# Copying the gather indices on GpSimd instead of ScalarE in the three walks of a graph network

## The reference

```python
z = (x @ W).reshape(num_nodes, heads, d)
e = leaky_relu(el[src] + er[dst])            # el, er: scores of z
alpha = softmax of e over the edges of one dst
out = jax.ops.segment_sum(z[src] * alpha[:, :, None], dst, num_segments=n)   # walk 1: 2 heads, walk 2: 1 head
...
msgs = x[src] * w[:, None]
agg = jax.ops.segment_sum(msgs, dst, num_segments=n)                         # walk 3
agg = agg / jnp.maximum(wsum, 1e-06)[:, None]
```

## Time and profile before

| | |
|---|---|
| median of 3 timed runs | 4649.5 us (4644.11 to 4653.87) |
| profiled execution: span, from first to last instruction | 5278.5 us |
| profiled execution: own time beside its span | none is given other than the span |
| mean granted TensorE clock, share of full speed | 0.746 |
| busy share of the span: PE, DVE, ACT, POOL | 59%, 37%, 29%, 51% |
| walks 1, 2, 3, the stretch that holds their gathers | 1252.7, 1190.7, 1179.0 us |
| gathers in each walk | 784 |

### The profile page before, as it was taken

How to read it: one execution, slowest core, us unless ns; L and a number is a source line. 1 busy time by engine, 2 the same in 40 slices (tenths; PEclk the granted TensorE clock), 3 DMA queues, 4 the chain that set the end, 5 groups by cost and what they waited for, 6 DMA issues and landing times. The chain is left out here.

```text
span 5278.5 us, 61729 instructions
## 1 busy us (share of the span) xinstructions
PE 3093.1 (59%) x11768; PEld 1898.6 (36%) x11768; DVE 1971.5 (37%) x5574; ACT 1533.2 (29%) x4863; POOL 2683.4 (51%) x2732
## 2 busy tenths in 40 slices
PE   3245555565543454455564499911666667666699
PEld 2123233333321222222233388810333333333466
DVE  4246565555523333333336712251222222223222
ACT  2122232222221222222222133310344443434233
POOL 0366666666626666666653145525666666661121
PEclk9667776767766777767775699965777777777899
DMA  5346566666623333333335266684444444442111
GB/s 152 84 97 104 107 107 109 106 110 106 107 53 97 98 95 97 99 96 97 99 87 150 76 204 218 223 234 125 118 118 122 120 122 120 123 121 60 63 57 49
DMA packets 381422, 598.24 MB, mean 113 GB/s; under 512 B 102442, under 2 KB 272078, under 8 KB 380658
## 3 DMA queue, kind: packets, MB, share of 16 engines
q0 software_dynamic: 136000, 386.29, 32.0%
q1 hardware_dynamic: 209138, 172.22, 12.1%
q10 hardware_dynamic: 36160, 38.56, 2.4%
HBM read 489.46 MB, written 107.34 MB: 113 GB/s over the span
## 5 line engine op out<-in xcount | busy, mean ns | idle before, releaser
L583 POOL DMA_INDIRECT walk_rows<-z_two_heads,walk_idx x784 | 793.6, 1012 | 523.3 <-ACT walk_idx L596 296.0
L583 POOL DMA_INDIRECT walk_rows<-z_one_head,walk_idx x784 | 762.9, 973 | 525.0 <-ACT walk_idx L596 296.7
L1874 POOL DMA_INDIRECT walk_rows<-h,walk_idx x784 | 746.7, 952 | 462.3 <-issue 234.1
L2019 PE MATMUL walk_ps_part<-walk_rows,walk_whot 128*80 128x257 f32 x1568 | 531.0, 475 | 207.1 <-issue 109.2
L730 PE MATMUL walk_ps_part<-walk_rows,walk_whot 128*80 128x257 f32 x1568 | 538.8, 492 | 1.1 <-issue 0.9
L730 PE MATMUL walk_ps_part<-walk_rows,walk_hot 128*80 128x258 f32 x1568 | 531.2, 472 | 0.2
L596 ACT ACTIVATE walk_idx<-keep_src 128x8 int32 x212 | 44.1, 208 | 1250.4 <-remote 942.6
L2019 PEld LDWEIGHTS walk_ps_part<-walk_rows,walk_whot 128*80 128x80 f32 x1568 | 263.1, 184 | 399.7 <-issue 359.3
L730 PEld LDWEIGHTS walk_ps_part<-walk_rows,walk_whot 128*80 128x80 f32 x1568 | 277.3, 193 | 184.3 <-issue 139.1
L730 PEld LDWEIGHTS walk_ps_part<-walk_rows,walk_hot 128*80 128x80 f32 x1568 | 257.2, 182 | 134.1 <-issue 75.4
L699 PE MATMUL walk_ps_row_scores<-keep_ident,walk_fmax 32*1 32x32 f32 (+1 forms) x98 | 18.6, 190 | 439.4 <-issue 234.6
(11 more groups left out here) (371 smaller groups left out, 5054.0 us busy)
## 6 DMA issues: line engine op xcount, KB each, us to landing
exp_w<-in_ffn_W SPq DMA_DIRECT2D x108, 512.0 KB
agg<-walk_window ACTq DMA_DIRECT2D x198, 80.3 KB
walk_rows<-z_two_heads,walk_idx POOLq DMA_INDIRECT x784
walk_rows<-z_one_head,walk_idx POOLq DMA_INDIRECT x784
comb_ya<-y_tokens POOLq DMA_DIRECT2D x28, 448.0 KB
walk_rows<-h,walk_idx POOLq DMA_INDIRECT x784
walk_erB<-er_two_heads SPq DMA_DIRECT2D x104, 80.0 KB
agg<-walk_window ACTq DMA_DIRECT2D x99, 80.6 KB
```

Source lines behind the costliest of these rows:

```text
L583: pool.indirect_dma_start(out=Z[k // 2][:, k % 2 * GROUP_TILES + t, :], out_offset=None, in_=table, in_offset=bass.IndirectOffsetOnAxis(ap ...
L1874: pool.indirect_dma_start(out=Z[k // 2][:, k % 2 * GROUP_TILES + t, :], out_offset=None, in_=table, in_offset=bass.IndirectOffsetOnAxis(ap ...
L2019: last = pe.matmul(P[k % 2][0:WIN, 0:HW], S[k % HOTS][:, t, :], Z[k // 2][:, k % 2 * GROUP_TILES + t, :], start=t == 0, stop=t == GROUP_TI ...
```

## The change

Index copies move from ScalarE to GpSimd in all three walks. In `gather` GpSimd now loads the group's number, waits until `idx[k]` is free, copies the 8 columns itself, waits for its own copy, then for the products of group s-8, and issues the 8 gathers. That `idx[k]` is free it takes from a count that tells that the gathers of group s-8 have landed: in `edge_walk` `el_turned4` (`el_turned` before, now started at 4, so VectorE's wait is moved by 4), which counts the pairs whose score columns were turned; in `mean_walk` the new `rows_seen8`, which the first product of each group increments. ScalarE loses `copy_idx`, the 8 copies at its start, and the load of the later group's number in `window`. Line numbers shift by a few: the gathers of walks 1 and 2 are L587, their index copy is L581.

```diff
 @block.gpsimd                      # edge_walk
-            def gather(s, k):
+            def gather(s, k, landed, count):
+                g = group(pool, s)
+                pool.wait_ge(landed, count)
+                pool.tensor_copy(idx[k][:, :], keep["src"][:, bass.ds(g * GROUP_TILES, GROUP_TILES)]) \
+                    .then_inc(idx_ready, 1)
+                pool.wait_ge(idx_ready, s + 1)
                 pool.wait_ge(done8, s + 1)
-                pool.wait_ge(idx_ready, s + 1)
                 pool.sem_inc(pool_tick, 1)
                 for t in range(GROUP_TILES):
                     pool.indirect_dma_start(
...
-            gather(0, 0)
-            gather(1, 1)
+            gather(0, 0, el_turned4, 1)
+            gather(1, 1, el_turned4, 1)
             with pool.Fori(0, n) as i:
                 for j in range(UNROLL):
-                    gather(i * UNROLL + (j + 2), (j + 2) % UNROLL)
+                    gather(i * UNROLL + (j + 2), (j + 2) % UNROLL, el_turned4, i * PAIRS + ((j + 2) // 2 + 1))
 @block.scalar
-            def copy_idx(g, k):
-                act.activation(idx[k][:, :], keep["src"][:, bass.ds(g * GROUP_TILES, GROUP_TILES)],
-                               ACT.Copy).then_inc(idx_ready, 1)
...
             def window(s, k, started):
-                n0, after = first_node(act, s), group(act, s + UNROLL)
+                n0 = first_node(act, s)
                 act.wait_ge(done8, s + (UNROLL + 1))
-                copy_idx(after, k)
...
-            for s in range(UNROLL):
-                copy_idx(group(act, s), s)
 @block.tensor
             pe.sem_inc(done8, UNROLL)
+            pe.sem_inc(el_turned4, PAIRS)
...
                 pe.transpose(psT[:, :], el, ident[:, :]) \
-                  .then_inc(el_turned, 1)
+                  .then_inc(el_turned4, 1)
 @block.vector
             def scan_el(p, q):
-                dve.wait_ge(el_turned, p + 1)
+                dve.wait_ge(el_turned4, p + (PAIRS + 1))
...
 @block.gpsimd                      # mean_walk: gather as above, with
+            gather(0, 0, rows_seen8, 1)
+            gather(1, 1, rows_seen8, 2)
...
+                    gather(i * UNROLL + (j + 2), (j + 2) % UNROLL, rows_seen8, i * UNROLL + (j + 3))
 @block.tensor                      # mean_walk
             pe.sem_inc(done8, UNROLL)
+            pe.sem_inc(rows_seen8, UNROLL)
...
+                    if t == 0:
+                        last.then_inc(rows_seen8, 1)
                     if t == GROUP_TILES - 1:
                         last.then_inc(done8, 1)
```

More of the change, by code:

```diff
@@ L498, in edge_walk @@
         inputs = [ph.sem(f"inputs{k}") for k in range(INS)]
-        (cols, inputs_used4, el_turned, ends_ready, ends_turned, ins_ready, ins_turned, max_ready, x_ready, w_ready,
+        (cols, inputs_used4, el_turned4, ends_ready, ends_turned, ins_ready, ins_turned, max_ready, x_ready, w_ready,
          sp_tick, row_tick) = (ph.sem(n) for n in (
-             "cols", "inputs_used4", "el_turned", "ends_ready", "ends_turned", "ins_ready", "ins_turned", "max_ready",
+             "cols", "inputs_used4", "el_turned4", "ends_ready", "ends_turned", "ins_ready", "ins_turned", "max_ready",
              "x_ready", "w_ready", "sp_tick", "row_tick"))
@@ L1744, in mean_walk @@
         gathered = [ph.sem(f"gathered{k}") for k in range(UNROLL)]
-        (idx_ready, local_ready, hot0_ready, hot_ready, scaled_ready, done8, win_ready2, stored, consts, pool_tick,
+        (idx_ready, local_ready, hot0_ready, hot_ready, scaled_ready, done8, rows_seen8, win_ready2, stored, consts, pool_tick,
          act_tick, pe_tick, dve_tick, sp_tick) = (ph.sem(n) for n in (
-             "idx_ready", "local_ready", "hot0_ready", "hot_ready", "scaled_ready", "done8", "win_ready2", "stored",
+             "idx_ready", "local_ready", "hot0_ready", "hot_ready", "scaled_ready", "done8", "rows_seen8", "win_ready2", "stored",
              "consts", "pool_tick", "act_tick", "pe_tick", "dve_tick", "sp_tick"))
```

## The result

The changed kernel takes 4834.4 us in the median of four runs (4834.3 to 4845.2), against 4651.6 for the kernel before in the same sitting: a ratio of 1.0406, 95% interval [1.0393, 1.0418]. It is 4.1% slower. Forecast were 4847 us and a range of 4620 to 4990.

The account below looks back on a forecast made before the run. The prediction took GpSimd's issue of gathers to bound the walks. From 4649.5 us, plus 235 for pauses, less 38 for earlier starts, it forecast 4847 us, 4.2% slower, with a range of 4620 to 4990.

Parts of the forecast that it names:

- the sum of the walks: All three walks: 294 groups, each with a pause of 0.80 us, add 235 us (182 to 368).
- GpSimd's issue bounds the walks: All three walks: GpSimd issues gathers without a pause, 985 us a walk.
- The stalls: Inside the profiled walks: 628.9 us of GpSimd waits are caused by the recording and absent from timed runs.
- The equal sums: Profile of before: waits of 628.9 us match the 629.0 between span and median, so timed runs lack them.
- The pause: Before each group's first gather: copy 0.30 plus hand-over 0.80 less the existing 0.30 gap, 0.80 us.
- The group load: GpSimd's group-number load in each group: runs in the waiting sequencer, costs nothing, at worst about 0.2 us.
- The early start: First gathers no longer wait for ScalarE: walk 1 gains 33.9 us, walk 3 4.1; 38 taken.
- ScalarE: Loses one 0.21 us copy and a group-number load per group; nobody waits for it, so nothing gained.
- VectorE's lock: Walks 1 and 2: VectorE operations with two SBUF inputs could lengthen GpSimd's copies, 17 us, left out of the sum.
- Rival 1: Inside the walks: the waits are real in timed runs, so the change is faster, 4543 us; chance 0.18.
- rival 2: Before each group's first gather: hand-over only 0.24 us, about 4656 us (4629 to 4682); chance 0.10.
- rival 3: Before each group's first gather: pause over 1.25 us, the copy starting slowly, above 4992 us; chance 0.02.

Follow-up runs that it names:

- before_psum: Kernel before, with VectorE first copying target scores to PSUM so its multiply L810 has one SBUF input: 4563.8 us, ratio 0.9814.
- one_ahead: Changed kernel, with GpSimd copying the indices of the next group ahead of this group's gathers: 4652.6 us, ratio 0.9989.
- own_memset: start_early, with GpSimd filling a spare tile and waiting for that fill before each group, ScalarE copying the indices: 4816.4 us, ratio 1.0336.
- after_psum: Changed kernel, with VectorE first copying target scores to PSUM so its multiply L810 has one SBUF input: 4787.5 us, ratio 1.0293.
- start_early: Kernel before, with ScalarE's first 8 index copies ahead of its wait for the weights in walks 1 and 3: 4622.8 us, ratio 0.9919.
- start_late: Changed kernel, with GpSimd waiting for the node weights of walks 1 and 3 before its first copy: 4891.8 us, ratio 1.0501.
- act_still: Changed kernel, with ScalarE still loading the later group's number and copying its indices into an unread spare tile: 4850.6 us, ratio 1.0412.
- before_again: Kernel before, unchanged, measured and profiled once more: 4661.9 us, span 4659.9 us.
- walk3_only: Kernel before with the changed kernel's whole mean_walk, so the change is in walk 3 alone: 4740.4 us, ratio 1.0178.

## Why the prediction was right

The mechanism held: GpSimd's issue sets the pace of the walks, and a copy of its own with a wait for it stops that issue once in every group. The forecast of 4847 us lies 13 above the measured time, and a part of that nearness is luck, as the sum of the walks shows.

- **GpSimd's issue bounds the walks.** Right. A walk was forecast at 985 us of gathers without a pause; `before_psum`, where nothing holds GpSimd, has 985.6, 985.5 and 982.1. Before, VectorE's holding came on top in walks 1 and 2 (78 and 18 us).
- **The stalls don't count.** The conclusion was right, the reason was not borne out. I took them for something the recording causes, and so forecast a span of 5200 to 5300 us for the changed kernel. It is 4832.6, and the second recorded execution of the kernel before spans 4659.9. The stalls came with one execution; what caused them there stays open. The equal sums (628.9 of waits against 629.0 of difference) were what could be relied on.
- **The pause.** 0.80 was taken, 0.74 measured: the copy 0.20 instead of 0.30, the hand-over 0.84 instead of 0.80. The 0.12 at the low end for the copy is the IOTA of the earlier trace rows; the 0.55 at the high end is shown by no run. The copies took 0.20 in the median and 0.89 at the longest, where VectorE held one. The gap in front of a group's first gather is 1.04 us, a little under the "1.1 us or more" that was to show it. `one_ahead` shows that the copy in itself costs only 0.06, `own_memset` that the wait costs nearly as much without the copy (0.67).
- **The sum of the walks.** Forecast 235, measured 229.8, and that they are so near is luck. `before_psum` and `after_psum`, without VectorE's holding, show what the pauses cost: 86.5 + 85.6 + 91.0 = 263 us. Of these 294 × 0.74 = 218 are the pause that was forecast; 33 × 0.81 = 27 are the once-a-turn gap and some 14 the slower gathers, and neither was in the sum. Against them stands what was not in the sum either: VectorE's holding shrinks with the change. In walk 1 it makes 1063.87 − 985.63 = 78 us before and 1119.92 − 1072.09 = 48 with the change, 30 less; in walk 2 it is 2 less.
- **The group load** was put at nothing, and that held: the copy, which needs the number, starts as the last gather ends. The once-a-turn gap is something else. `own_memset` has it without a load on GpSimd, and the stalled first trace of before has it in walk 3 (a step of 2.08, 11 times) without a copy on GpSimd. The second trace of before, where GpSimd's groups follow each other without a wait, has none. So it goes with waits that end GpSimd's lead; what fills it stays open.
- **The early start.** Forecast 38. The traces show 36.5 − 3.0 in walk 1, and in walk 3 the copy behind the weights gone; `start_early` measures 36, `start_late` 44.
- **ScalarE.** Forecast at nothing, and `act_still` shows nothing.
- **VectorE's lock** was left out of the sum at 17 us for the copies. It is 10.7 on the copies. The estimate had a reading wrong: L870 multiplies rows by `walk_ps_work`, which is in PSUM, so it has one input from SBUF, not two. With L810 alone the same formula gives 7 us in walk 1 and 3 in walk 2. The larger part of the holding, on the gathers, was in the kernel before already and shrank.
- **Rival 1** (the waits are real) falls with `before_again`; **rival 2** (a hand-over of 0.24) holds only where a copy waits, not a gather; **rival 3** (over 1.25 us a group) falls with the 0.74.

What doesn't add up from the walks: 229.8 less 38 is 192, while the spans differ by 172.7. The other 19 us lie outside the walks: the stage before walk 1 is 8.1 us shorter in the changed kernel's trace, and from the last gather of walk 1 to the first of walk 2 it is 88.5 us instead of 97.9. Both differ between executions whose code is the same there: VectorE's first instruction of walk 1 stands at 175.05 in the earlier trace rows and at 179.66 in `start_early`, and the second stretch takes 89.8 us in `walk3_only`, where walks 1 and 2 are those of before. So they are not put down to the change.

## What to carry to other kernels

An engine that sets the pace by running its queue without a pause should not wait for a result that it has just made: in this kernel the price was not the small instruction (0.06 us) but the hand-over to the next one (0.84 us in front of a gather), paid each time, and with the engine's lead gone a further gap of 0.81 us showed in each turn of the loop. Make the result one step earlier, or leave it to an engine that has time. Before moving work to "the engine that waits", see in a second execution whether it waits at all: the waits of the first profile were in no other execution on record here.

## What was not expected of the hardware

- Gathers on GpSimd are held by a VectorE multiply with two inputs from SBUF. A gather that starts inside one ends 0.83 us after the multiply in the median, only 0.12 less than a whole free gather takes, and moving one input to PSUM brought 90 us (1.9%). The Trainium skill (SBUF — State Buffer, "Who interferes with whom") reports that such a multiply did not stall DMAs issued on GpSimd, because it takes only the read interface of the shared port pair, while making descriptors needs the write interface (it calls this reason inferred). For gathers, which read their indices from SBUF, the measurement decides: they are held. That it is the reading of the indices was not tried by itself. For copies on GpSimd the trace agrees with the lock that the Trainium skill states in the same section for a GpSimd instruction that reads SBUF (0.85 us instead of 0.20).
- GpSimd's wait for its own result costs 0.17 us in front of a copy and 0.84 to 0.91 in front of a gather. The Trainium skill (GPSIMD Engine Reference, "Instruction dispatch") says that completion holds back only what waits for the instruction's semaphore, not the next instruction. The trace agrees: without such a wait a gather follows a copy after 0.16 us.
- In the kernels where GpSimd copies the indices in all three walks, its other gathers are slower by about 0.01 us in walk 3 (1.262 to 1.264 from start to start against 1.251, medians over the 686 gathers that aren't the first of a group), some 8 us; in walks 1 and 2 it is half as much. It is not the copying as such: with fills instead of copies they are not slower (1.251), and neither in `walk3_only`, where GpSimd copies in walk 3 (1.252). The cause stays open.
